# Cross-attention on one core: small per-row arithmetic in one-tensor forms, DMA stores issued ahead of loads, memory subtractions in halves, and 24 large subtractions moved from GpSimd to VectorE

## The reference, cut to what matters

```python
memory_proj = jnp.einsum('bme,de->bmd', memory, W_mem)
scores = jnp.einsum('bnd,bmd->bnm', hidden_states, memory_proj) / jnp.sqrt(jnp.float32(D))
attn = jax.nn.softmax(scores, axis=-1)
memory_context = jnp.einsum('bnm,bmd->bnd', attn, memory_proj)
gate_input = jnp.concatenate([hidden_states, memory_context], axis=-1)
gate = jax.nn.sigmoid(jnp.einsum('bnf,df->bnd', gate_input, W_gate) + b_gate)
fused = hidden_states + gate * memory_context
return _rmsnorm(fused, norm_w)
```

## Time and profile before

| | |
|---|---|
| median of 3 runs | 1566.95 us (1565.29 to 1569.71) |
| profiled execution, its own time | 1563.07 us |
| span of the profiled execution | 1561.2 us |
| TensorE busy | 1503.3 us (96% of the span), 6528 matmuls |
| VectorE busy | 1205.2 us (77%) |
| ScalarE busy | 654.7 us (42%) |
| GpSimd busy | 308.1 us (20%) |
| attention stage | 533.84 to 1244.06 us of the span |

### The profile page before, as it was taken

The page is one execution under the profiler, slowest core; times in us unless marked ns, Lnnn a source line. Parts: engine busy times, 40 slices in busy tenths (PEclk is TensorE's granted clock), DMA queues, the critical chain, the costliest instruction groups (busy, mean ns, idle before and its releaser), DMA issues.

```text
span 1561.2 us, 20134 instructions
## 1 busy us (share of the span) xinstructions
PE 1503.3 (96%) x6528; PEld 1227.8 (79%) x6528; DVE 1205.2 (77%) x1567; ACT 654.7 (42%) x1009; POOL 308.1 (20%) x263
## 2 busy tenths in 40 slices
PE   7999999999999999999998998899999999999997
PEld 6888888888888777788777886688778878888886
DVE  6565768777777878886687767886687999988987
ACT  4333242222222366335644366335644444444443
POOL 0000000000000663208322274106422001110011
PEclk9999999999999999999999999999999999999998
DMA  9999436333334467862887367863779444555553
GB/s 187 222 238 215 127 97 166 111 111 107 107 107 121 103 201 220 196 153 92 230 219 165 100 180 203 198 156 100 216 206 218 128 163 189 190 195 198 198 200 122
DMA packets 231181, 259.80 MB, mean 166 GB/s; under 512 B 34769, under 2 KB 178129, under 8 KB 230865
## 3 DMA queue, kind: packets, MB, share of 16 engines
q1 hardware_dynamic: 231120, 259.06, 59.4%
HBM read 170.92 MB, written 85.98 MB: 165 GB/s over the span
## 4 chain that ended last, share of the span: by engine, by line
PE 34%; DVE 11%; POOL 7%; DMA 6%; issue 4%; ACT 2%; SPq 2%; DVEq 0%; ACTq 0%; POOLq 0%
PE banks L2120 19%; PE banks L1947 12%; PE banks L2040 3%; POOL region_l L802 3%; DMA prob_scratch<-prob 2%; DVE region_l L392 2%; DMA region_f<-q_scratch 2%; DMA am_scratch<-am_out 1%; DVE half_max L1559 1%; DVE region_t L392 1%; DVE region_n L392 1%; DVE banks L1613 1%; DMA region_f<-prob_scratch 1%; POOL region_f L791 1%; DVE region_f L1523 1%
## 5 line engine op out<-in xcount | busy, mean ns | idle before, releaser
L1947 PE MATMUL banks<-region_t,region_n 128*128 128x512 f32 x960 | 219.7, 391 | 8.6 <-DVE region_n L392 7.3
L1947 PEld LDWEIGHTS banks<-region_t,region_n 128*128 128x128 f32 x960 | 181.1, 189 | 46.8 <-DVE region_t L392 9.0
L782 POOL TENSOR_TENSOR region_f<-region_f 128x1024 f32<-128x1024 f32 x23 | 60.1, 2622 | 735.4 <-DVE region_f L1523 630.1
L392 DVE TENSOR_TENSOR region_t<-region_f,region_t 128x1024 fp32r<-128x1024 f32 (+2 forms) x87 | 141.2, 1639 | 69.5 <-ACT region_t L882 57.3
L1947 PE MATMUL banks<-region_t,region_l 128*128 128x512 f32 x768 | 180.2, 396 | 7.3 <-DVE region_l L392 7.2
L1947 PE MATMUL banks<-region_n,region_l 128*128 128x512 f32 x768 | 177.1, 392 | 4.0 <-DVE region_l L392 3.9
L1947 PEld LDWEIGHTS banks<-region_t,region_l 128*128 128x128 f32 x768 | 146.9, 192 | 39.9 <-DVE region_l L392 9.0
L1947 PEld LDWEIGHTS banks<-region_n,region_l 128*128 128x128 f32 x768 | 145.0, 189 | 35.4 <-DVE region_l L392 5.2
L1994 PE MATMUL banks<-region_t,region_l 128*128 128x512 f32 x576 | 135.8, 389 | 0.0
L2040 PE MATMUL banks<-region_t,region_l 128*128 128x512 f32 x480 | 118.0, 394 | 11.6 <-DVE banks L1585 4.3
L1081 ACT CAST region_l<-banks 128x512 fp32r<-128x512 f32 x128 | 73.7, 586 | 124.3 <-DVE banks L1613 90.1
(11 more groups left out here) (129 smaller groups left out, 2412.1 us busy)
## 6 DMA issues: line engine op xcount, KB each, us to landing
region_f<-in_ctx SPq DMA_DIRECT2D x128, 256.0 KB, 5.4
region_f<-prob_scratch SPq DMA_DIRECT2D x160, 128.0 KB, 5.0
region_f<-in_x SPq DMA_DIRECT2D x64, 256.0 KB, 5.7
region_f<-in_x SPq DMA_DIRECT2D x128, 128.0 KB, 2.7
prob_scratch<-prob SPq DMA_DIRECT2D x32, 512.0 KB, 5.1
prob_scratch<-region_f SPq DMA_DIRECT2D x32, 512.0 KB, 3.3
region_f<-in_x SPq DMA_DIRECT2D x16, 1024.0 KB, 4.9
out<-region_f SPq DMA_DIRECT2D x31, 512.0 KB, 2.6
```

Source lines behind the costliest of these rows:

```text
L392: return nc.vector.tensor_tensor(dst, src, hi.bitcast(F32), ALU.subtract)
L782: nc.gpsimd.tensor_tensor(dst, a, b, ALU.subtract).then_inc(mt_sum, 1)
L1947: mm = nc.tensor.matmul(dst, lhs(a), rhs(b), start=first and n == 0, stop=last and n == len(PASSES) - 1)
```

## The change

Four edits, all in the attention stage, and reorderings that go with them.

1. *Row maxima and weights.* `half_max` and `run_max` are gone. The maximum is written to `neg_max`, then scaled in place; for h=1 one `tensor_scalar` multiplies it by -SCALE and takes the minimum with the column of h=0. `weights_of_halves` works on single columns by `tensor_scalar` with per-row scalars, beside one reciprocal of 128x2. The exponential of the difference (`weight_exp`) is done per unit on ScalarE, right behind the exponential of each unit of h=1.
2. *SyncE's order.* In batches 1 to 3 the probability stores of pairs k=2 and k=3 of h=0 are issued ahead of the memory loads, and memory tile 3 is loaded after the stores of pair k=0 of h=1. Query tile 2 is loaded ahead of the raw memory tile of batch 0.
3. *Memory subtractions.* `mn_lo` (128x2048) is done as two of 128x1024, for tiles 1 and 2 one half in slot 0 and one in slot 1.
4. *Left subtractions.* Group 2 (128x1024, 24 in all) goes from GpSimd's `q_lo` to VectorE's new `q_mid`, with a semaphore of its own. One 128x1024 subtraction of batch 0 (`w_sums(1, 1)`) moves to VectorE too, and GpSimd's `w_sums(H + 1, 4)` goes behind the query work of pair k=3.

Further: ScalarE's `first_half` goes behind the splits of groups 1 and 2 of the next unit; the subtraction of group 1 and transpose of group 2 of the first unit go behind `add_last`.

```diff
+        NWT = 5
             load_raw(1, 0)
-            sp.wait_ge(mt_ready, 6)
-            load_raw(1, 1)
             for i in range(3):
                 sp.wait_ge(zx_stored[i], 16 * NPAIR)
             load_q(2)
+            sp.wait_ge(mt_ready, 6)
+            load_raw(1, 1)
...
             q_sums(0)
-            q_lo(0, 1, 2)
-            q_lo(0, 3)
+            q_lo(0, 1, 3)
...
                     q_lo(L, 3)
-                    q_lo(L + 1, 1, 2, 3)
+                    q_lo(L + 1, 1, 3)
                     q_sums(L + 2)
-                    q_lo(L + 2, 1, 2, 3)
+                    q_lo(L + 2, 1, 3)
+                    q_sums(L + 3)
+                    q_lo(L + 3, 1, 3)
                     w_sums(H + 1, 4)
-                    q_sums(L + 3)
-                    q_lo(L + 3, 1, 2, 3)
...
+                if h:
+                    nc.scalar.activation(weight[:, unit:unit + 1], neg_max[:, unit:unit + 1], ACT.Exp,
+                                         bias=neg_max[:, UPB + unit:UPB + unit + 1], scale=-1.0).then_inc(wt_exp, 1)
...
-                first_half(b, i)
                 if following:
                     pt_hi_of(b, i + 1, 1)
                     pt_hi_of(b, i + 1, 2)
+                first_half(b, i)
...
                 if h:
-                    nc.vector.tensor_tensor(run_max[:, unit:unit + 1], m, half_max[:, unit:unit + 1], ALU.max
-                                            ).then_inc(run_done[u], 1)
-                    dve.wait_ge(run_done[u], PPB * b + k + 1)
-                    m = run_max[:, unit:unit + 1]
-                nc.vector.tensor_scalar(neg_max[:, col:col + 1], m, -SCALE, None, ALU.mult).then_inc(neg_ready[u], 1)
+                    nc.vector.tensor_scalar(m, m, -SCALE, neg_max[:, unit:unit + 1], ALU.mult, ALU.min
+                                            ).then_inc(neg_ready[u], 1)
+                else:
+                    nc.vector.tensor_scalar(m, m, -SCALE, None, ALU.mult).then_inc(neg_ready[u], 1)
...
+                for u in range(2):
+                    unit = 2 * pair + u
+                    nc.vector.tensor_scalar(half_sum[:, unit:unit + 1], weight[:, unit:unit + 1],
+                                            half_sum[:, unit:unit + 1], half_sum[:, UPB + unit:UPB + unit + 1],
+                                            ALU.mult, ALU.add).then_inc(wt_step, 1)
...
+            def q_mid(L):
+                dve.wait_ge(uq_hi, 3 * L + 2)
+                v = left_group(L, 2)
+                minus_hi(v[:, LO], q_group(L, 2), v[:, HI]).then_inc(uq_mid, 1)
...
+                        if k < 3 and n == 1:
+                            q_mid(L + k + 1)
...
-                        mn_lo(b, 0)
-                    if k in (1, 2) and n == 1:
-                        mn_lo(b, k)
+                        mn_lo(b, 0, 0, 1)
+                    if k in (1, 2) and n < 2:
+                        mn_lo(b, k, n)
+                        if n == 1:
+                            q_mid(L + 3 + k)
...
-                        pt_transpose(b, 0, 2)
-                        pt_lo_of(b, 0, 1)
...
+                    if i == 6:
+                        if b < NB - 1:
+                            q_mid(LPB * (b + 1))
...
                 add_last(b, 1, PPB - 1)
+                pt_lo_of(b, 0, 1)
+                pt_transpose(b, 0, 2)
```

More of the change, by code:

```diff
@@ L1632, in weights_of_halves @@
+                sums = [half_sum[:, UPB * h + 2 * pair:UPB * h + 2 * pair + 2] for h in range(2)]
+                for u in range(2):
[3 more added lines that the diff above has]
+                                            ALU.mult, ALU.add).then_inc(wt_step, 1)
                 dve.wait_ge(wt_step, NWT * Q + 2)
-                nc.vector.reciprocal(inverse, total).then_inc(wt_step, 1)
+                nc.vector.reciprocal(sums[1], sums[0]).then_inc(wt_step, 1)
@@ L1634, in weights_of_halves @@
                 dve.wait_ge(wt_step, NWT * Q + 3)
-                nc.vector.tensor_tensor(scaled, w, inverse, ALU.mult).then_inc(wt_step, 1)
+                for u in range(2):
+                    unit = 2 * pair + u
+                    nc.vector.tensor_scalar(weight[:, unit:unit + 1], weight[:, unit:unit + 1],
+                                            half_sum[:, UPB + unit:UPB + unit + 1], None, ALU.mult
+                                            ).then_inc(wt_step, 1)
             def join_halves(b, i):
-                A, col = UPB * b + i, 2 * UPB + am_unit(0, i)
+                A, col = UPB * b + i, UPB + am_unit(0, i)
@@ L1797, in memory_first @@
                     w_sums(0, 3, 4)
+                if i == 5:
+                    q_mid(0)
                 if i == 6:
```

132 lines of the change are left out of this document (64 added, 68 removed).

## The result

| | before | after |
|---|---|---|
| median | 1566.95 us | 1519.89 us (1518.58 to 1521.87) |
| profiled execution | 1563.07 us | 1521.87 us |

The ratio is 0.9699, interval 0.9671 to 0.9727: faster by 47 us. The direction and the places were right, the size was not.

A forecast was written before the change was run, and what follows sets the result against it. TensorE was taken as the bound, losing 57.3 us in the attention stage. Gains of 18.2 + 10.5 + 4.5 - 2.4 = 30.8 us from the 1566.95 us median gave 1536 us, range 1525 to 1553.

The forecast's parts named there:

- memory stages: Attention's memory stages: small operations no longer held by GpSimd, 19.1 us regained less 0.9 for `q_mid`, 18.2 us gained.
- the clock: Scoring, batches 1 to 3: half clock behind waits for memory tile 1, one and a third falls, 2.4 us lost.
- scoring 0: Batch 0's scoring: VectorE overfull, `add_last` late three times; 4.5 us gained of 12.9 lost, bounds -2 and 9.
- 761.04: Scoring, batches 1 to 3: `keep_22`'s store wait goes, memory tile 1 comes late instead; gain taken as 0.
- transposed probabilities: Scoring, batches 1 to 3: they land some 2 us later behind a full queue; 0.9 us lost, times 3.
- 742.00: Scoring, batches 1 to 3: ScalarE's copy, late behind GpSimd's LO subtraction and `w_sums`, is freed; about 1.0 us gained, times 3.
- 778.84: Scoring, batches 1 to 3: `close_0`, late behind a 128x2048 subtraction, is freed by halving it; 1.15 us gained, times 3.
- 800.49: Scoring, batches 1 to 3: `add_last` no longer stands behind a transpose and a split; 1.0 us gained, times 3.
- only the memory stages gain: Rival: each scoring wait turns into another, so only the 18.2 us come; 1549 us, chance 0.23.
- `q_mid` holds `close_0`: Rival: in scoring slot 1 `q_mid` makes `add_last` 1.2 us late in 23 pairs, 27.6 us; 1576 us, chance 0.06.
- new forms still held: Rival: weights operations still wait for GpSimd's subtractions, 2.3 us each, in the memory stages; about 1564 us, chance 0.05.
- One for one: Rival: new waits replace the old ones, within 0.3% of before; 1565 us, chance 0.05.

The follow-up runs named there:

- alone again: The changed kernel, unaltered, measured again on another chip against the kernel before: median 1518.71 us, ratio 0.9703.
- both delays back: The changed kernel with the two-tensor forms and `first_half` ahead of the splits again, against the kernel before: ratio 0.9853.
- tile 1 early: The changed kernel with memory tile 1 of batches 1 to 3 loaded ahead of the store of pair k=3, unit 0: 1517.82 us, ratio 0.9706.
- the two moves: The kernel before with SyncE's new order and `first_half` behind the splits, no arithmetic changed: ratio 0.9796.

## Why the prediction was too small

The direction and most of the places were right. The size failed on one term of the scoring stages, SyncE's order, and the cause given for the memory stages was half of it.

| step | forecast | profile after | alone again |
|---|---|---|---|
| memory stages | 18.2 | 19.1 | 19.1 |
| scoring 1 to 3, with the clock | 10.5 - 2.4 = 8.1 | 17.1 | 20.1 |
| scoring 0 | 4.5 | 5.5 | 6.0 |
| sum | 30.8 | 41.7 | 45.2 |

- **The step that failed is the one on SyncE's order in batches 1 to 3.** It was sized at 0 us at 761.04 (old waits against the late tile), 0.9 lost three times at the transposed probabilities, and 2.4 lost to the clock: 5.1 us lost. Undoing the order shows 8.3 us gained. That is 13.4 us, nearly all of the 14.4 us between the forecast's sum and the second profile. The tile's course was right: forecast to be issued 39.9 us into the stage and to land 9.4 us later, it was issued at 39.4 (744.17 - 704.81) and used at 49.4. What was wrong is the step from ScalarE to TensorE: ScalarE waited 3.40 us, TensorE only 1.82, and 0.50 and 1.15 in the other batches, because `seed_b` had slack (0.89, 0.79 and 0.70 in the second profile); the charge was three times 2.5. On the other side, the waits that the new order saves are not the 2.6 to 2.9 us per batch of the kernel before, but larger in the changed kernel: 2.0 to 2.6 us for `keep_22` alone, against 1.0 to 1.4. The 8.3 us hold one fall of the clock in the kernel with the old order, worth under 2 us; without it the term is still off by over 11 us. On the kernel before, the order alone gives these stages 9.5 us. No loss came at tile 3, and the clock fell once in one profile and not in the other, where 1.3 falls were charged.
- **The other small waits of scoring** (742.00, 778.84, 787.05, 800.49) were put at 13.2 us; 20.1 - 8.3 = 11.8 us came. Good in size, partly wrong in cause: moving work off GpSimd was not what freed 742.00, and halving the memory subtraction was not needed at 778.84. The wait at 800.49 is gone with SyncE's order alone, though a transpose and a split still stand ahead of `add_last` there: the move that the prediction paid for it is not needed either. Such waits have more than one cure, so the 11.8 us can't be shared out among the edits.
- **Memory stages**: 19.1 us, all of it, as forecast, and `q_mid` in slot `late` cost nothing where 0.9 was set aside. The reason was half of it. The held additions are one of two delays in series, and the other, `first_half` waiting for its store, was booked as "gives VectorE more". It takes 17 us by itself. Had edit 1 been forecast without that move, 19.1 would have been too much: the forms alone left 3.6 us.
- **Batch 0**: 7.4 us of loss remain where 8.4 were expected, with `add_last` late at 548.95 and 569.88 by 1.20 and 1.09 us, as said, and at 559.00 by 0.28 only. VectorE was busy for 75.9 us there, not 82.2, and for 60 in the later stages, not 65: edit 1's forms alone had taken it from 74.9 to 70.3 and from 59.1 to 55.1 us, more than the prediction gave back for the holds.
- **The base**: forecast from the median with a difference taken from profiles. It holds for the second pair: 45.2 us by profile, 46.5 by ratio. The first profile alone would have given 41.7 us against 47, since it fell on the slowest of its three runs and that of the kernel before on the fastest.
- **Rivals**: *only the memory stages gain* is refuted by 17 to 20 us in scoring; *`q_mid` holds `close_0`* by scoring that is the same with and without it (242.0 and 242.3 us); *new forms still held* by their times, 0.44, 0.17 and 0.34 us beside GpSimd. That rival was the case under the Trainium skill's rule on two-port modes (SBUF — State Buffer, "Who interferes with whom"), which is for operands that meet the conditions of such a mode: for operations of one and two columns no effect of that rule is seen. *One for one* needs no more. The low end of the range, 1525, stood next to "all named waits gone", 1526. By the prediction's own terms that is 19.1 for the memory stages and 3 x 7.2 for scoring, some 41 us, and leaves out the 4.5 us of batch 0: with them it is 1522. The time came below the range because batch 0 gave 5.5 to 6.0 us on top of nearly all the named waits.

## What to carry to other kernels

Follow a wait back past the first slow operation, until something is on time: here a second delay of 5 us ended 6 us upstream of the slow addition, and either fix took most of the gain, so that neither's worth can be read from the sum. Ask of every wait on a store what is queued ahead of it; moving the instruction that waits behind work that doesn't need it was worth 17 us here. Where a term has two opposite parts, charge each from its own rows rather than set them to zero against one another.

## What was not expected of the hardware

Half clock behind a wait: all eight waits of 3.3 to 3.4 us of these profiles (before, SyncE's order alone, both delays back) were followed by some us at half the granted clock, 1.2 instead of 2.4 GHz; the 3.3 to 3.5 us right behind each show a mean granted clock of 0.50 to 0.70. Behind waits of 1.8 to 2.6 us it went either way: in the changed kernel behind the 1.82 us at 757.93, not behind the 1.83 us at 537.66; with tile 1 early behind that one; not behind 2.47 us at 607.68 in SyncE's order alone, but behind 2.53 at the same place in the two moves (1.00 and 0.56 over the next 3.3 us). So a 3.4 us wait costs nearer 5 us, and taking away half of it may take away the fall too. Two kernels that differ by one wait of this kind can't be told apart by a single profile: the changed kernel's two attention stages differ by 3.5 us.
